# Expert routing placed later in each step, and layer 0's deviations taken from the attention's variance

## The chip, the cores and the metric

The kernel runs on one core of a Trainium2 chip. The time is the device time of one execution in microseconds (us); of several runs the median is given. The engines are TensorE (PE in the rows, PEld for its weight loads), VectorE (DVE), ScalarE (ACT), GpSimd (POOL) and SyncE (SP), each with a queue of its own that it works off in order; they wait for one another by semaphores.

## The reference

128 batches of 32 tokens with 128 channels go through three sublayers, each with a residual sum: a cross-attention to 257 context tokens (16 heads), a self-attention over the 32 tokens (16 heads), and a stack of four mixture-of-experts layers. The last is what the change touches:

```
def moe_layer(x, rw, rb, g, b, w1, b1, w2, b2):      # 4 experts, hidden 512, top 2
    logits = x @ rw + rb
    vals, idx = top_k(softmax(logits), 2);  vals = vals / vals.sum()
    xhat = (x - mean(x)) * rsqrt(var(x) + 1e-5)
    h = gelu((xhat * g[e] + b[e]) @ w1[e] + b1[e])
    y = h @ w2[e] + b2[e]
    return sum over chosen e of vals[e] * (x + y[e])
x = x2 + layers(layernorm(x2))                        # x2: what the self-attention leaves
```

Layer 0's input is itself a layer norm of x2: its mean is zero and its variance is that of x2 scaled by the square of the first inverse deviation.

## The kernel before

The 4096 tokens are 32 tiles of 128 (NT), eight blocks of four tiles (NBLK). The kernel has three parts one after the other, each an `nc.Block` whose end all engines wait for: cross-attention, self-attention, experts. All products with 16-bit operands are made of parts: a value is split into a high half and a low half (`xh` and `xl`, `gh` and `gl`, weights with parts 0 and 1), and three products make one.

The expert part runs over 32 steps (NSTEP): layer 0's eight blocks, then layer 1's, and so on. A step has four units e = 0 to 3, one for each expert. `steps` calls each engine's `unit(u, v, f, third, e, final)`: u is the current unit, v the unit before it (its second products and its combination are done one unit late), f the next step (what it needs is prepared now), third the step after that. The order of the calls in `unit` is the order of each engine's queue.

TensorE in a unit: `hidden(u)` (12 products of 512 columns, L1846); at e = 1 the transposes of the next step's normalised tokens (L1877); at e = 2 the twelve small routing products of the next step (L1887), which wait for `xl`; at e = 3 the second bias (L1896); then `outputs(v)` (48 products of 128 columns, L1863); at e = 1 the transpose of the combine weights (L1902).

ScalarE in a unit: four Gelus (L1666) and two copies to `gh` (L1671); at e = 1 `xh` (L1676); at e = 3 the tanh of the routing (L1690); in the first steps also `attended` (L1071), which writes the expert stack's input `hs` of one tile from the attention's output `xs`, and `high_weights` (L1036, L1039).

GpSimd makes half of `gl` (L1649), VectorE the other half (`low_half`, L1731).

VectorE in a unit: at e = 0 `normalise` (xc, L1719; in layer 3 also hs + xs, L1725); at e = 1 `deviations(third)` (statistics L1705 and L1709, then the inverse square root by three Newton steps, L38 to L53) and `xl` (L1812); `low_half(u)`; at e = 2 `route(f)` (L1755 to L1781, 14 small instructions in a chain, the last writes z); `combine(v)` (L1745, four instructions into hs); at e = 3 `add_bias` (L1801) and `weigh(f)` (L1784 to L1794). In steps 1 to 6 two experts' weights are split (`low_weights`, L1046 and L1050), behind e = 2 and e = 3, and TensorE waits ahead of step 7 (`ready`) until all are. (`outputs(v)` of e = 3 runs in the next step's e = 0.)

At the end of the self-attention part VectorE takes the statistics of the first eight attended tiles (`st8`, `mv8`), normalises the first block, splits the weights of experts 0 and 1, and then runs `attended_late` (the attention's deviations of the last eight tiles, L1426 to L1429) and the bias sum b1c (L1435).

## Time and profile before

| what | value |
|---|---|
| runs | 1383.1, 1382.77, 1380.51 us; median 1382.77 |
| profiled execution | 1380.24 us |
| its span, first to last instruction | 1378.5 us |
| mean granted TensorE clock | 0.97 |
| TensorE busy | 1270.3 us (92%) |
| VectorE busy | 1203.2 us (87%) |
| ScalarE busy | 1128.8 us (82%) |
| GpSimd busy | 714.0 us (52%) |

Busy times are shares of the whole span; which engine sets the end is read stage by stage. The expert part begins near 630 us. All rows are of the one profiled execution, which is 2.5 us under the median of the runs.

### The profile page before, as it was taken

The numbers are of one execution on the slowest core, as the hardware profiler recorded it, in microseconds if no ns is written. First come the engines' busy times: TensorE is split into PE (matmuls) and PEld (weight loads), VectorE is DVE, ScalarE is ACT, GpSimd is POOL, SyncE is SP. The second block draws the span as 40 slices with busy tenths as digits, with TensorE's granted clock in tenths as the row PEclk, the third lists the DMA queues.
The fourth block names the chain that finished last, engine by engine and source line by source line (L and its number), as shares of the span: only waits on it lengthen the run. The fifth ranks groups of instructions, "written<-read, shape, count | busy, mean of one in ns | idle before, by whom it ended". The sixth has DMA issues, their size and how long they took to land. (4 is left out here: it accounts for less than half of the span.)

```text
span 1378.5 us, 41462 instructions
## 1 busy us (share of the span) xinstructions
PE 1270.3 (92%) x15611; PEld 966.0 (70%) x15611; DVE 1203.2 (87%) x3492; ACT 1128.8 (82%) x1931; POOL 714.0 (52%) x559
## 2 busy tenths in 40 slices
PE   5898999999997689997889979999999999999998
PEld 3576778777776578954567657777777777776776
DVE  4799989999998678977899979998999999999986
ACT  3598999999996656766899968888888888888886
POOL 7276777777776864542334333344333344444343
PEclk9999999999998679999999999999999999999999
DMA  5985676676663279820000000000000000000000
GB/s 157 240 217 156 191 184 183 188 189 183 191 183 86 49 198 209 216 53 1 2 2 2 2 1 2 2 2 2 2 2 2 2 2 2 2 10 17 10 17 17
DMA packets 196269, 109.41 MB, mean 79 GB/s; under 512 B 89740, under 2 KB 194028, under 8 KB 196076
## 3 DMA queue, kind: packets, MB, share of 16 engines
q1 hardware_dynamic: 122032, 84.65, 22.1%
q10 hardware_dynamic: 74044, 22.17, 7.3%
q8 instruction: 123, 2.02, 0.6%
q14 instruction: 70, 0.57, 0.2%
HBM read 67.62 MB, written 39.03 MB: 77 GB/s over the span
## 5 line engine op out<-in xcount | busy, mean ns | idle before, releaser
L1649 POOL TENSOR_TENSOR gl<-gf,gh 128x1024 f16<-128x1024 f32 x128 | 290.6, 2270 | 461.7 <-ACT gh L1671 461.7
L1666 ACT ACTIVATE gf<-pair,b1c 128x512 f32<-128x512 f32 x512 | 329.5, 680 | 77.1 <-PE pair L1846 76.9
L1863 PE MATMUL pair<-w2p,gh 128*128 128x128 f16 x4096 | 356.9, 219 | 4.3 <-DVE hs L1745 2.6
L1863 PE MATMUL pair<-w2p,gl 128*128 128x128 f16 x2048 | 349.7, 219 | 0.0
L1846 PE MATMUL pair<-xh,w1p 128*128 128x512 f16 x1024 | 328.3, 382 | 7.3 <-DVE w1p L1046 7.3
L405 POOL TENSOR_TENSOR pl<-p,ph 128x1024 f16<-128x1024 f32 x128 | 273.1, 2134 | 116.0 <-ACT ph L462 115.9
L1863 PEld LDWEIGHTS pair<-w2p,gh 128*128 128x128 f16 x4096 | 317.5, 98 | 20.8 <-DVE hs L1745 3.1
L1671 ACT ACTIVATE gh<-gf 128x1024 f16<-128x1024 f32 x256 | 270.6, 1057 | 23.6 <-ACT gf L1666 0.4
L1731 DVE SCALAR_TENSOR_TENSOR gl<-gf,gh 128x1024 f16<-128x1024 f32 x128 | 164.0, 1281 | 42.0 <-ACT gh L1671 41.5
L1863 PEld LDWEIGHTS pair<-w2p,gl 128*128 128x128 f16 x2048 | 200.3, 98 | 0.0
L1846 PE MATMUL pair<-xl,w1p 128*128 128x512 f16 x512 | 195.7, 382 | 0.0
L1846 PEld LDWEIGHTS pair<-xh,w1p 128*128 128x128 f16 x1024 | 100.9, 99 | 115.3 <-DVE w1p L1046 7.4
L461 ACT ACTIVATE p<-pair 128x512 f32<-128x512 f32 x256 | 158.0, 617 | 23.7 <-PE pair L867 21.2
L462 ACT ACTIVATE ph<-pair 128x512 f16<-128x512 f32 x256 | 160.2, 626 | 0.0
L769 DVE TENSOR_REDUCE mx<-pair 128x4 f32<-128x1024 f32 x128 | 154.0, 1203 | 1.5 <-PE pair L840 0.5
L1745 DVE SCALAR_TENSOR_TENSOR hs<-pair,comb,hs 128x128 f32<-128x128 f32 x512 | 143.0, 339 | 0.1
L890 PE MATMUL pair<-VX,ph 128*128 128x36 f16 x1024 | 92.2, 180 | 9.1 <-DVE sl L630 6.2
L890 PEld LDWEIGHTS pair<-VX,ph 128*128 128x128 f16 x1024 | 83.7, 97 | 20.7 <-issue 14.5
L891 PE MATMUL pair<-VX,ph 128*128 128x36 f16 x1024 | 91.5, 179 | 0.0
L892 PE MATMUL pair<-VX,pl 128*128 128x36 f16 x1024 | 91.5, 179 | 0.0
L820 PE MATMUL pair<-cT,WkT 128*128 128x512 f32 x128 | 72.4, 648 | 20.2 <-ACT cT L452 12.6
L867 PE MATMUL pair<-QS,KS 98*128 98x128 f16 x1024 | 82.8, 224 | 4.0 <-ACT ph L462 3.4
(252 smaller groups left out, 2458.0 us busy)
## 6 DMA issues: line engine op xcount, KB each, us to landing
KS<-k_parts_dram SPq DMA_DIRECT2D x64, 384.0 KB, 4.5
k_parts_dram<-kh SPq DMA_DIRECT2D x64, 256.0 KB, 3.3
cx<-in_ctx_dram ACTq DMA_DIRECT2D x30, 512.0 KB, 4.7
k_parts_dram<-kl SPq DMA_DIRECT2D x64, 128.0 KB, 3.6
w1p<-in_L_ffn_w_dram SPq DMA_DIRECT2D x8, 512.0 KB, 6.0
w2p<-in_L_ffn_w_dram SPq DMA_DIRECT2D x8, 512.0 KB, 8.0
QS<-q_parts_dram ACTq DMA_DIRECT2D x128, 24.0 KB
K<-k_parts_dram SPq DMA_DIRECT2D x8, 384.0 KB
```

The source lines that it names most:

```text
L405: pool.tensor_tensor(pl[n % 4][:, :, :], p32[n % 2][:, :, :], ph[n % 4][:, :, :], ALU.subtract).then_inc(pl_done, 1)
L461: act.activation(p32[n % 2][:, c, :], TB[:, c * 512:(c + 1) * 512], ACT.Exp)
L462: act.activation(ph[n % 4][:, c, :], TB[:, c * 512:(c + 1) * 512], ACT.Exp).then_inc(t_read[c], 1)
L769: dve.tensor_reduce(mx[n // PB % 2][:, :, n % PB], RB[:, :].rearrange("p (g k) -> p g k", g=G), AX.X, ALU.max, negate=True).then_inc(r_rea ...
L890: pe.matmul(o, p_hi, hi, start=(c == 0), stop=False)
L1649: pool.tensor_tensor(gl[u.m2][:, 0:h, :], gf[u.m2][:, 0:h, :], gh[u.m2][:, 0:h, :], ALU.subtract).then_inc(d_loP, 1)
L1666: act.activation(gf[u.m2][:, c, :], hb[c][:, :], ACT.Gelu, scale=1.0 / WS, bias=b1c[:, u.step.expert(u.e), c]).then_inc(d_g, 1)
L1671: act.activation(gh[u.m2][:, c - 1:c + 1, :], gf[u.m2][:, c - 1:c + 1, :], ACT.Copy).then_inc(d_hi, 1)
L1731: dve.scalar_tensor_tensor(gl[u.m2][:, h:FC, :], gf[u.m2][:, h:FC, :], 1.0, gh[u.m2][:, h:FC, :], ALU.mult, ALU.subtract).then_inc(d_loD, 1)
L1745: dve.scalar_tensor_tensor(t, yb[v.m2][:, k * D:(k + 1) * D], comb[v.step.m2][:, k, v.e:v.e + 1], t, ALU.mult, ALU.add).then_inc(d_acc, 1)
L1846: last = pe.matmul(hb[c][:, :], w1p[:, u.step.expert(u.e), part, c * P:(c + 1) * P].rearrange("p a f -> p (a f)"), x[k][u.step.m2][:, :], ...
L1863: last = pe.matmul(yb[v.m2][:, t * D:(t + 1) * D], g[:, c, t * P:(t + 1) * P], w2p[:, le, part, c, :].rearrange("p a h -> p (a h)"), start ...
```

## The change

1. **Order on TensorE.** At e = 2 the routing products stand behind `outputs(v)` and not ahead of it.
2. **Order on VectorE.** `combine(v)` stands ahead of `route(f)`.
3. **Layer 0's deviations.** VectorE no longer takes statistics of the attended tiles. `expert_scale` works the deviation out of the attention's variance and inverse deviation, for 24 tiles in step (7, 3) of the attention part, for the last 8 in step 2 of the experts. `normalise_first` makes xc from `xs` with one combined scale. `late_deviations` (the attention's own for the last 8 tiles) moves into step 1.
4. **Attended tiles.** Tiles 16 to 31 are written by VectorE (`attended_late`, four tensor_scalars at e = 3 of steps 2 to 5) and no longer by ScalarE; ScalarE does 0 to 15.
5. **xh and xl of step 0** are made inside the attention part.
6. **Weights.** One expert's weights are split a step, steps 1 to 12 (ScalarE behind e = 0, VectorE behind e = 3); TensorE waits for a layer's weights at its first block, and `ready` is gone.
7. **Last layer.** hs + xs is made by GpSimd behind its `gl` of e = 0.

```diff
+        def expert_scale(dve, own, base):
+            dve.wait_ge(e_ln, base)
+            dve.scalar_tensor_tensor(vE[:, own], mv3[:, own, 1], 1.0, rs3[:, own], ALU.mult, ALU.mult).then_inc(e_ln, 1)
+            dve.wait_ge(e_ln, base + 1)
+            dve.scalar_tensor_tensor(vE[:, own], vE[:, own], 1.0, rs3[:, own], ALU.mult, ALU.mult).then_inc(e_ln, 1)
+            dve.wait_ge(e_ln, base + 2)
+            inverse_deviation(dve, seed, rsE[:, own], rwE[:, own], rt3[:, own], vE[:, own], e_ln, base + 2)
+            dve.scalar_tensor_tensor(rrE[:, own], rs3[:, own], 1.0, rsE[:, own], ALU.mult, ALU.mult).then_inc(e_ln, 1)
+        def normalise_first(dve, n):
+            dve.wait_ge(e_ln, SCALED if 4 * n + 4 <= HEAD else LATE_SCALED)
+            wait(dve, d_xT, n)
+            for k in range(4):
+                t = 4 * n + k
+                dve.tensor_scalar(xc[:, k, :], xs[:, t, :], mv3[:, t, 0:1], rrE[:, t:t + 1],
+                                  ALU.subtract, ALU.mult).then_inc(d_x, 1)
...
                             if at == (NBLK, 0):
-                                dve.wait_ge(d_hs, 8)
-                                for k in range(8):
-                                    dve.bn_stats(st8[:, k, :], hs[:, k, :]).then_inc(d_ln, 1)
...
+                                normalise_first(dve, 0)
+                                for le in range(2):
+                                    dve.wait_ge(e_b1, le + 1)
+                                    low_weights(dve, le)
+                            if at == (NBLK, 2):
+                                tokens_low(dve, 0)
...
                     blocks(step, prepare)(dve)
-                    dve.wait_ge(c_st, 2 * NT)
-                    attended_late()
...
-                        if splits and split and e in split_units:
-                            split(eng, 2 * cur.n + (E - 2 + split_units.index(e)))
+                        if split and cur and 1 <= cur.n <= LE - E and e == split_unit:
+                            split(eng, E - 1 + cur.n)
...
+                        if u and f and final and e == 0:
+                            blk = slice(4 * f.block, 4 * f.block + 4)
+                            pool.wait_ge(d_x, 4 * f.n + 4)
+                            pool.tensor_tensor(hs[:, blk, :], hs[:, blk, :], xs[:, blk, :], ALU.add).then_inc(d_sum, 1)
...
+                    def attended_late(n):
+                        dve.wait_ge(e_ln, LATE_R if 4 * n + 4 > HEAD else HEAD + RSTD_STEPS + 1)
+                        for t in range(4 * n, 4 * n + 4):
+                            dve.tensor_scalar(hs[:, t, :], xs[:, t, :], mv3[:, t, 0:1], rs3[:, t:t + 1],
+                                              ALU.subtract, ALU.mult).then_inc(d_hs, 1)
...
                         if u and f and e == 0:
-                            normalise(f, final)
-                        if u and third and e == 1 and not opening:
+                            if f.layer == 0:
+                                normalise_first(dve, f.n)
+                            else:
+                                normalise(f)
+                        if third and e == 1 and third.layer:
                             deviations(third)
...
-                        if opening and e == 2:
-                            deviations(third)
+                        if v:
+                            combine(v)
                         if f and e == 2:
                             route(f)
-                        if v:
-                            combine(v, final)
                         if u and e == 3:
                             add_bias(u.step)
                         if at == (0, 1):
                             low_weights(dve, 3)
+                        if at == (1, 2):
+                            late_deviations()
+                        if at == (2, 2):
+                            expert_scale(dve, slice(HEAD, NT), LATE_R)
+                        if u and e == 3 and 2 <= u.step.n < 6:
+                            attended_late(u.step.n + 2)
...
-                    steps(dve, unit, low_weights, (2, 3), lead=True)
+                    steps(dve, unit, low_weights, 3, lead=True)
...
+                        if v:
+                            outputs(v)
                         if f and e == 2:
...
-                        if v:
-                            outputs(v)
...
-                    def weights_ready():
-                        pe.wait_ge(e_lo1, LE)
-                        pe.wait_ge(e_lo2, LE)
-                    steps(pe, unit, ready=weights_ready)
+                    steps(pe, unit)
```

## Rows read from the trace of the kernel before

**Rows 1.** Windows: busy us and instructions of each engine, granted clock, DMA
```profile
640.00:820.00 180.00, 159.93 (x1812) 113.99 (x1810) 160.49 (x498) 153.88 (x232) 66.56 (x29) 0.98 0.01 2
820.00:1176.00 356.00, 355.88 (x4129) 260.04 (x4127) 325.71 (x1029) 308.04 (x433) 140.69 (x65) 1.00 0.01 2
1176.00:1378.00 202.00, 192.41 (x2250) 141.21 (x2247) 176.63 (x523) 164.24 (x230) 81.08 (x35) 1.00 0.04 12
```

**Rows 2.** Waits of TensorE from 600 us: total, times, longest
```profile
PE pair L1887 <- DVE xl L1812: 14.0, 14, 5.9
PE pair L1846 <- DVE w1p L1046: 7.3, 1, 7.3
...
PE pair L1863 <- DVE hs L1745: 2.6, 1, 2.6
```

**Rows 3.** Timeline, L1902 alone: start, us, instruction, idle before it
```profile
642.54 0.23 PE L1902 MATMUL pair<-ident,c 128*128 128x128 f16 x1 [1.52 <-DVE c L1794]
...
667.62 0.22 PE L1902 MATMUL pair<-ident,c 128*128 128x128 f16 x1
...
717.88 0.22 PE L1902 MATMUL pair<-ident,c 128*128 128x128 f16 x1
...
788.39 0.22 PE L1902 MATMUL pair<-ident,c 128*128 128x128 f16 x1
...
820.75 0.22 PE L1902 MATMUL pair<-ident,c 128*128 128x128 f16 x1
...
842.84 0.22 PE L1902 MATMUL pair<-ident,c 128*128 128x128 f16 x1
...
1176.92 0.22 PE L1902 MATMUL pair<-ident,c 128*128 128x128 f16 x1
...
1360.47 0.22 PE L1902 MATMUL pair<-ident,c 128*128 128x128 f16 x1
```

**Rows 4.** Timeline around the start of the expert part, and one window
```profile
625.14 0.64 DVE L1426 BATCH_NORM_AGGREGATE mv<-st 128x2 f32<-128x6 f32 x8
...
628.30 0.26 DVE L1435 TENSOR_TENSOR b1c<-pair,cols 128x64 f32<-128x64 f32 x1
...
629.56 0.69 DVE L1812 TENSOR_TENSOR xl<-pair,xh 128x512 f16<-128x512 f32 x1 [0.53 <-ACT xh L1676]
...
630.31 0.21 PE L1887 MATMUL pair<-rwp,xh 128*128 128x4 f16 x2 [5.94 <-DVE xl L1812]
...
632.00:634.00 2.00, 2.00 (x6) 0.64 (x5) 1.83 (x10) 1.39 (x3) 0.00 (x0) 0.50 0.00 0
```

**Rows 5.** Timeline of VectorE and GpSimd in one step at the floor
```profile
852.28 1.93 DVE L1781 SCALAR_TENSOR_TENSOR z<-top,lg 128x16 f32<-128x16 f32 x1
...
855.16 1.21 DVE L1731 SCALAR_TENSOR_TENSOR gl<-gf,gh 128x1024 f16<-128x1024 f32 x1
...
858.13 1.57 DVE L1784 TENSOR_SCALAR sel<-sel 128x16 f32<-128x16 f32 x1
...
860.25 1.24 DVE L1719 TENSOR_SCALAR xc<-hs,mv,rs 128x128 f32<-128x128 f32 x4
...
852.04 2.13 POOL L1649 TENSOR_TENSOR gl<-gf,gh 128x1024 f16<-128x1024 f32 x1 [3.33 <-ACT gh L1671]
857.52 2.14 POOL L1649 TENSOR_TENSOR gl<-gf,gh 128x1024 f16<-128x1024 f32 x1 [3.36 <-ACT gh L1671]
```

**Rows 6.** Timeline of VectorE in step 6: deviations and the second split
```profile
787.25 0.86 DVE L1705 BATCH_NORM_STATS2 st<-hs 128x6 f32<-128x128 f32 x4
...
790.92 0.69 DVE L1812 TENSOR_TENSOR xl<-pair,xh 128x512 f16<-128x512 f32 x1
...
806.14 0.74 DVE L1046 SCALAR_TENSOR_TENSOR w1p<-w1p,gain 128x512 f16<-128x512 f32 x1
...
807.41 1.11 DVE L1719 TENSOR_SCALAR xc<-hs,mv,rs 128x128 f32<-128x128 f32 x4
```

**Rows 7.** Timeline of VectorE in layer 3: the sum with xs
```profile
1173.22 0.69 DVE L1725 TENSOR_TENSOR hs<-hs,xs 128x512 f32<-128x512 f32 x1
```

More of the change, by code:

```diff
@@ L1060, in build @@
         e_rwh, e_b2, e_ln = sem("e_rwh"), sem("e_b2"), sem("e_ln")
[L1061 to L1063 removed]
+        vE, rsE, rwE, rrE = (sb(whole, f"rsE_{i}", [P, NT], F32) for i in range(4))
+        xh = [sb(whole, f"xh{i}", [P, 4 * P], F16) for i in range(2)]
+        xl = [sb(whole, f"xl{i}", [P, 4 * P], F16) for i in range(2)]
         warm = sb(whole, "warm", [P, 1], F32)
@@ L1526, in _ @@
                     blocks(step)(pe)
-                    pe.wait_ge(d_x, 4)
-                    pe.wait_ge(c_oc, NT)
-                    for k in range(4):
-                        last = pe.transpose(bank[6][:, k * P:(k + 1) * P], xc[:, k, :], ident[:, :])
-                    last.then_inc(d_xT, 1)
                     pe.wait_ge(e_cols, 5)
@@ L1590, in __init__, with steps, run @@
                     self.step, self.e, self.n, self.m2 = step, e, step.unit + e, e % 2
-            def steps(eng, unit, split=None, split_units=(0, 2), ready=None, lead=False):
-                SPLITS = (LE - E) // 2
-                def run(it, c, final, prepare=True, attend=True, splits=False, moments=lead):
+            def steps(eng, unit, split=None, split_unit=0, lead=False):
+                def run(it, c, final, prepare=True, attend=True, moments=lead):
                     cur = Step(eng, it, c) if attend else None
@@ L1620, in steps @@
                 run(0, 0, False)
-                for s in range(1, 1 + SPLITS):
-                    run(0, s, False, splits=True)
-                if ready:
-                    ready()
-                for s in range(1 + SPLITS, NSTEP - 2):
+                for s in range(1, NSTEP - 2):
                     run(0, s, s >= LAST - 1)
@@ L1738, in combine @@
                         dve.wait_ge(d_comb, v.step.n + 1)
-                        if final and v.e == 0:
-                            due = v.step.n - LAST + 2
-                            dve.wait_ge(d_sum, min(due, NBLK) if isinstance(due, int) else due)
+                        if v.step.layer == 0 and v.e == 0:
+                            dve.wait_ge(d_hs, 4 * v.step.n + 4)
+                        if v.step.layer == L - 1 and v.e == 0:
+                            dve.wait_ge(d_sum, v.step.block + 1)
                         for k in range(4):
@@ L1839, in hidden @@
                             pe.wait_ge(d_xl, u.step.n + 1)
-                        if isinstance(u.n, int) and u.n in (2, 3):
-                            pe.wait_ge(e_lo1, u.n + 1)
+                        if u.step.block == 0:
+                            pe.wait_ge(e_lo1, E * u.step.layer + u.e + 1)
                         x = (xh, xl, xh)
@@ L1852, in outputs @@
                         le = v.step.expert(v.e)
-                        if isinstance(v.n, int) and v.n in (2, 3):
-                            pe.wait_ge(e_lo2, v.n + 1)
+                        if v.step.block == 0:
+                            pe.wait_ge(e_lo2, E * v.step.layer + v.e + 1)
                         for c in range(FC):
@@ L1878, in unit @@
                             last.then_inc(d_xT, 1)
+                        if u and e == 3:
+                            if f:
+                                pe.wait_ge(d_xl, f.n + 1)
+                            pe.wait_ge(d_cc, u.step.n + 1)
+                            pe.matmul(tbk[:, :], cT16[:, :], b2R[:, bass.ds(u.step.layer, 1), :].rearrange("p a m -> p (a m)"),
+                                      start=True, stop=True).then_inc(d_P, 1)
+                        if v:
+                            outputs(v)
                         if f and e == 2:
```

137 lines of the change are left out of this document (59 added, 78 removed).

## The prediction

> **What bounds the kernel now.** I read the busy time by stretch first, then who waited for whom on TensorE, then the starts of one TensorE instruction that occurs once a step, and last the VectorE, GpSimd and ScalarE rows of one step. The expert stage (step 0 to step 31, four expert units a step) is TensorE's: between 820 and 1176 us it is busy 355.9 of 356 us, while VectorE has 325.7 [rows 1]. Before and after that it is not full: 159.9 of 180 us in layer 0, 192.4 of 202 us from layer 3 to the end [rows 1]. The longest waits of TensorE are all put down to VectorE [rows 2].
>
> The transpose of the combine weights (L1902) gives the step times [rows 3]. From 842.84 to 1176.92 it is 15 steps, 22.27 us each: TensorE's own work, the floor. Layer 0, 642.54 to 842.84, takes 200.3 us for 8 steps, 22.1 over their floor of 178.2. Step by step: 25.08 for step 0 (2.8 over), 50.26 for steps 1 and 2 (5.7 over), 70.51 for 3 to 5 (3.7 over), 32.36 for step 6 (10.1 over), about 0 for step 7. Layer 3, 1176.92 to 1360.47, takes 183.55, 5.4 over. So 27.5 us is all that VectorE's schedule costs, and the change can't win more there. The start of the stage is a second place: the attention block ends with VectorE's late deviations (625.14 to 628.3) and bias sum, and TensorE's first routing product waits 5.94 us for xl until 630.31; its clock is then granted at 0.50, the 1.2 GHz level, until 634 at least [rows 4].
>
> **The start.** The change takes `attended_late` out of the block's end: 625.14 to 628.30, 3.2 us on VectorE [rows 4]. It puts in `expert_scale` (15 instructions of 0.2 to 0.25: 3.0 to 3.7 us) and moves both `low_weights` and the first normalisation ahead. By the order in the code VectorE then reaches the last tile's transpose some 2.5 us later than now, the b1 products follow it, and the bias sum ends near 625.8 instead of 628.56. Since xh and xl of step 0 are now made inside the block, the 629.56 xl [rows 4] leaves the path: the routing product comes some 0.35 us after the bias sum, near 626.2, 4.1 us earlier. The gap ahead of it shrinks from 5.9 us to about 1 us, so the clock should stay at 2.4 GHz; at 0.50 it cost half of 630.3 to 634, about 2 us of products. ScalarE has one weight split ahead of its first Gelu instead of a split and four tiles. The first L1902 waits for VectorE's c16 now and will again. I take 6 us earlier for it (bounds 4.5, and 7.4 with the clock's 2 us and the ScalarE work counted in full).
>
> **The order in a step.** In a step at the floor the row of z (L1781) lasts 1.93 us, from 852.28 to 854.21, and GpSimd's gl runs 852.04 to 854.17; sel (L1784) lasts 1.57, from 858.13 to 859.70, and the next gl ends at 859.66 [rows 5]. Alone, each takes 0.2. So VectorE's small instructions are held until GpSimd's subtraction is over, some 3.1 us a step. The Trainium skill says this as a rule (SBUF — State Buffer, "Who interferes with whom"): a VectorE instruction with two SBUF inputs or in a two-port mode and a GpSimd instruction block each other for the whole instruction; the rows agree.
>
> Now put `combine` (1.04 us) ahead of `route` (2.7 us of work). Routing starts near 850.8, GpSimd starts at 852.04, the rest of the chain is held to 854.2 and ends near 855.2. The two together end where they end now (low_half starts at 855.16), because routing meets the same hold; only z is 1.0 us later. Tanh waits for it, the next Gelu comes 0.5 us late, with it GpSimd's gl and the end of sel's hold. xc (L1719), at 860.25 now, then starts near 860.7 and ends near 861.9; TensorE wants it at about 862.0. So the reordering alone costs nothing in a step without extras: I take 0.1 us for each of steps 13 to 23, +1 (bounds 0, and 4 if the 0.5 shows in most steps). What it wins is the wait for xl at the routing product (14.0 us over 14 waits, 5.94 of them the first [rows 2]), since the product now comes 2.7 us later, and step 0's 2.6 us wait for hs, where routing and deviations stood ahead of combine.
>
> **Layer 0.** From steps 0 to 5 the deviations go (787.25 to 790.92: 3.7 us each [rows 6]) and one of two weight splits (806.14 to 807.41: 1.27 us [rows 6]). Added: `late_deviations` in step 1 (3.1 us, as 625.14 to 628.30 less nb), `expert_scale` in step 2 (3.0), and in steps 2 to 5 `attended_late`, four tensor_scalars like xc, 1.04 us. In sum VectorE has 4 us a step less to do. But what is added stands at e = 2 and 3, ahead of low_half(3) and xc, and the deviations left from e = 1, where VectorE then waits for ScalarE. So the position counts, not the sum:
> - Step 1: routing ends near 854.8 in the times of the row step, late deviations 857.9, low_half(3) 859.0; TensorE wants it at about 858.1, then xc one split later: 2.0 us lost.
> - Step 2: expert_scale ends as gl starts and low_half(3) is held to 859.7: 2.9 lost, then attended_late and split put xc 2.0 later: 4.9.
> - Steps 3 to 5: attended_late stands where sel stands, at 858. If held like sel it ends at 860.5, then weights 0.75 and split 1.27 put xc at 862.5 to 863.6: 1.6 lost. If it slips through, 0.6. I take 1.5, since the held sel is a tensor_scalar too [rows 5]: 4.6 for three.
> - Steps 6 and 7: deviations are back, with one split: xc at 860.7 + 1.27 ends at 863.1: 1.0 lost each. But `ready`, the wait for all splits (7.3 us [rows 2], the 10.1 of step 6 with the slow clock after it), is gone, as weights are wanted a layer at a time.
> Sum with 0.3 for step 0: 13.8 against 22.1, so -8.3 (bounds: 4 lost if nothing is held, 19 if all is, so -18 to -3).
>
> **Steps 8 to 12** have a split each that they have not now: 5 x 1.0 = +5 (bounds 0, and 7 at more than the split's own 1.27).
>
> **Layer 3.** The sum with xs leaves VectorE: 0.69 us [rows 7], which is the 0.7 by which these steps exceed the floor. On GpSimd it is half of a 2.13 us instruction [rows 5], 1.07, right after xc, where it delays gl and holds VectorE's deviations by up to 0.4 to 0.8. I take 0.4 a step: 3.2 against 5.4, -2.2 (bounds 1 and 7 lost, -4.4 to +1.6). The Trainium skill speaks against this edit (GPSIMD Engine Reference, "Engine selection"): a two-input elementwise operation is about twice as slow there; by it the add would take 1.4 us and the gain would be near 1.
>
> **Sum.** -6 - 8.3 + 5 + 1 - 2.2 = -10.5 us against the profiled execution's 1380.24 (span 1378.5 and 1.7 around it), so 1369.7. The median of the runs is 1382.77, 2.5 above it; in that measure 1372.2.
>
> **Rivals.**
> 1. *VectorE's slack is real* (24 in 100): the added work slides into time in which VectorE would be held anyway, splits cost 0.3, steps 0 to 12 lose 8 in all. Then -7 at the start and 8 + 3 us left of 27.5, so -16.5: -23.5 in all, 1359 in the median's measure. For it: 4 us less work a step, and 325.7 of 356 us busy includes the holds. Against: steps 3 to 5 now lose 1.23 each (3.7 by three) with a plain chain of this kind.
> 2. *The split on the chain decides, slower* (8 in 100): the split now stands once between weigh and xc in steps 1 to 12 with nothing to hide it. At 1.0 a step it costs 12 us; if a step over the floor is also held longer at both places, it is 2.0 or more for steps 3 to 12, 20 us, plus 10 for steps 1 and 2 and 7 in layer 3: 37 against 27.5, less 5 at the start: 1387 (1380.2 + 4.5 + 2.5). It decides from 1.6 us a step.
> 3. *No change that shows* (8 in 100): the same losses as now, the start gains 3 and steps 8 to 23 give it back: 1382. Below 0.2% (2.8 us) a measurement of this kernel can't tell.
> 4. My own case, 1366 to 1379, has 60.
>
> **Numbers.** 1372. Eight in ten between 1357 and 1382. Faster by over 0.2%: my case and the first rival, 84 in 100; same 8; slower 8.
>
> **What would show it.** The first L1902 near 636.5; no wait of w1p on the first product of layer 0's last step; no wait of L1887 for xl; steps 1 and 2 at 24 to 27 us; steps 3 to 12 at 23 to 24 with the wait at L1877 for xc; 22.3 from step 13 on; 22.7 in layer 3, GpSimd's add near 1.07 us. I am wrong if steps 3 to 12 stand at 22.3 (rival 1) or above 24 (rival 2), or if routing is not held by gl in its new place.

## The result and the profile after

The changed kernel takes 1410.51 us (median of four runs, 1410.05 to 1413.83), the kernel before in the same job 1381.67 (1380.51 to 1383.1): a ratio of 1.0218, interval 1.02 to 1.0236. It is 28.8 us slower; 10.5 us faster was forecast.

The profiled execution has a span of 1408.3 us, 29.8 more than before. From the page of the changed kernel, its busy times and the group of GpSimd's gl (busy us, mean ns, idle before):

```profile
span 1408.3 us, 41350 instructions
...
PE 1281.9 (91%) x15611; PEld 977.5 (69%) x15611; DVE 1230.3 (87%) x3367; ACT 1119.5 (79%) x1915; POOL 731.6 (52%) x567
...
L1653 POOL TENSOR_TENSOR gl<-gf,gh 128x1024 f16<-128x1024 f32 x128 | 291.7, 2279 | 459.7 <-ACT gh L1680 459.7
```

The starts of the transpose of the combine weights (now L1924) answer to [rows 3]; they are steps 0, 1, 2, 3, 4, 5, 6, 8, 13, 23, 24 and 25. The last, step 31, is at 1390.28.

```profile
637.45 0.23 PE L1924 MATMUL pair<-ident,c 128*128 128x128 f16 x1 [1.67 <-DVE c L1811]
659.82 0.22 PE L1924 MATMUL pair<-ident,c 128*128 128x128 f16 x1
687.64 0.22 PE L1924 MATMUL pair<-ident,c 128*128 128x128 f16 x1
718.56 0.22 PE L1924 MATMUL pair<-ident,c 128*128 128x128 f16 x1
746.52 0.22 PE L1924 MATMUL pair<-ident,c 128*128 128x128 f16 x1
774.03 0.22 PE L1924 MATMUL pair<-ident,c 128*128 128x128 f16 x1
803.07 0.22 PE L1924 MATMUL pair<-ident,c 128*128 128x128 f16 x1
...
850.38 0.22 PE L1924 MATMUL pair<-ident,c 128*128 128x128 f16 x1
...
973.98 0.22 PE L1924 MATMUL pair<-ident,c 128*128 128x128 f16 x1
...
1200.74 0.22 PE L1924 MATMUL pair<-ident,c 128*128 128x128 f16 x1
1225.59 0.22 PE L1924 MATMUL pair<-ident,c 128*128 128x128 f16 x1
1248.44 0.22 PE L1924 MATMUL pair<-ident,c 128*128 128x128 f16 x1
```

Against the same steps of before: the start is 5.1 us earlier; steps 0 to 7 take 212.9 us (200.3 before), steps 8 to 12 123.6 (111.4), steps 13 to 22 226.8 (222.7), layer 3 189.5 (183.6). That is -5.1 + 12.6 + 12.2 + 4.1 + 6.0 = +29.8. Of these stretches only the start won. Within the first, step 0 (22.37 for 25.08) and step 6 (23.32 for 32.36) gained as forecast, and steps 1 to 5 lost more than that. The same four stretches as windows, and the waits in the expert part that matter (in all, times, longest), which answer to [rows 1, 2]:

```profile
637.45:850.38 212.93, 187.77 (x2065) 137.83 (x2066) 176.16 (x463) 164.60 (x240) 70.42 (x32) 0.95 0.01 2
850.38:973.98 123.60, 114.05 (x1294) 82.93 (x1292) 116.44 (x346) 99.98 (x144) 47.94 (x20) 0.99 0.01 2
973.98:1200.74 226.76, 224.36 (x2583) 162.57 (x2581) 211.65 (x643) 189.92 (x270) 95.14 (x41) 1.00 0.01 2
1200.74:1390.28 189.54, 178.08 (x2063) 130.00 (x2061) 174.78 (x489) 152.54 (x216) 86.51 (x40) 1.00 0.04 11
```

```profile
ACT th L1694 <- DVE z L1798: 34.9, 30, 1.4
...
PE pair L1885 <- DVE gl L1742: 22.4, 24, 3.9
...
PE pair L1899 <- DVE xc L1089: 15.6, 4, 4.2
PE pair L1899 <- DVE xc L1720: 10.5, 7, 3.3
```

The waits for xl and for w1p are gone, as forecast. In their place TensorE waits for gl (VectorE's low_half) and for xc, some of these waits 3 to 4 us long. No wait of TensorE or ScalarE names GpSimd's gl. The first row is ScalarE's: its tanh now waits for z in nearly every step, where before it did so twice (4.5 us in all). Step 4 (746.52 to 774.03) shows why the long ones are so long. Its timeline in order of time, of VectorE (the three small rows between sel and w1p are left out), GpSimd and the TensorE row that waited, and then the windows around it:

```profile
761.52 2.14 POOL L1653 TENSOR_TENSOR gl<-gf,gh 128x1024 f16<-128x1024 f32 x1 [3.80 <-ACT gh L1680]
761.78 2.73 DVE L1735 TENSOR_SCALAR hs<-xs,mv,rs 128x128 f32<-128x128 f32 x4
764.43 0.16 DVE L1801 TENSOR_SCALAR sel<-sel 128x16 f32<-128x16 f32 x1
...
765.15 0.74 DVE L1046 SCALAR_TENSOR_TENSOR w1p<-w1p,gain 128x512 f16<-128x512 f32 x1
765.81 0.68 DVE L1050 SCALAR_TENSOR_TENSOR w2p<-w2p 128x512 f16<-128x512 f32 x1
766.41 3.07 DVE L1089 TENSOR_SCALAR xc<-xs,mv,rsE 128x128 f32<-128x128 f32 x4
767.25 2.15 POOL L1653 TENSOR_TENSOR gl<-gf,gh 128x1024 f16<-128x1024 f32 x1 [3.59 <-ACT gh L1680]
...
769.54 1.11 PE L1899 MATMUL pair<-ident,xc 128*128 128x128 f32 x4 [3.89 <-DVE xc L1089]
```

```profile
766.00:768.00 2.00, 0.00 (x0) 0.00 (x0) 2.00 (x5) 1.91 (x4) 0.75 (x1) 1.00 0.00 0
768.00:770.00 2.00, 0.46 (x2) 0.46 (x3) 2.00 (x2) 1.38 (x2) 1.40 (x1) 0.73 0.00 0
770.00:772.00 2.00, 2.00 (x19) 1.93 (x18) 2.00 (x6) 0.60 (x1) 0.00 (x0) 0.50 0.04 8
772.00:774.00 2.00, 2.00 (x36) 2.00 (x34) 1.39 (x2) 0.00 (x0) 0.00 (x0) 0.92 0.00 0
```

GpSimd runs ahead of VectorE here: its gl of the next step's unit 0 starts at 761.52 and ends at 763.66, while VectorE is at the end of e = 3. The late attention outputs (L1735), 1.0 us of work, last 2.73: the first of the four is held. That was foreseen. sel, c16 and the split follow without a hold, and xc starts at 766.41. But ScalarE's chain doesn't wait for xc: it releases GpSimd's next gl, that of unit 1, which starts at 767.25, while the four instructions of xc are under way. They last 3.07 instead of 1.11. So xc is ready not 1.6 us late but 3.9 us, and after TensorE stood for these 3.89 us its clock is granted at 0.50, the 1.2 GHz level, in 770 to 772; the rows return to 0.92 in the next two. The step takes 22.27 + 3.89 + 1.35 = 27.51; the 1.35 is the rest, and the windows account for it: 2.00 us at 0.50, 2.00 at 0.92, and the 0.46 busy in the window before, if that was at 0.50 too, are some 1.4 us lost. In step 5 the clock is below 1.00 for longer and the rest is 2.9. Waits of 3.88, 3.13 and 3.68, 4.15, 3.89, 3.89 and 3.29 us stand in steps 1, 2, 3, 4, 5 and 12, and waits of 1.01 in step 6 and 1.24 in steps 7 to 11, where xc ends before the next gl starts (at 871.13, gl at 871.77, in step 8).

### The profile page after: what moved, and what is told of

Read it like the earlier page. It is cut to its first block, busy times and chain, and to the rows that moved or that the text cites. A ratio compares the mean times of both kernels' runs of the same rounds, so it can differ in the third digit from the quotient of the medians.

```text
span 1408.3 us, 41350 instructions
## 1 busy us (share of the span) xinstructions
PE 1281.9 (91%) x15611; PEld 977.5 (69%) x15611; DVE 1230.3 (87%) x3367; ACT 1119.5 (79%) x1915; POOL 731.6 (52%) x567
## 3 DMA queue, kind: packets, MB, share of 16 engines
q1 hardware_dynamic: 122032, 84.65, 21.6%
## 4 chain that ended last, share of the span: by engine, by line
DVE 20%; PE 19%; ACT 9%; issue 5%; POOL 1%; DVEq 0%; ACTq 0%
PE pair L1885 10%; PE pair L1868 8%; ACT gf L1675 5%; ACT gh L1680 4%; DVE hs L1756 3%; DVE ge L1785 2%; DVE gl L1742 2%; POOL gl L1653 1%; DVE xc L1720 1%; DVE sel L1801 1%; DVE xc L1089 1%; DVE gt L1788 1%; PE pair L1899 1%; DVE hs L1735 1%; DVE w2p L1050 1%
## 5 line engine op out<-in xcount | busy, mean ns | idle before, releaser
L1885 PE MATMUL pair<-w2p,gh 128*128 128x128 f16 x4096 | 367.3, 221 | 22.5 <-DVE gl L1742 22.4
L1675 ACT ACTIVATE gf<-pair,b1c 128x512 f32<-128x512 f32 x512 | 325.7, 677 | 63.0 <-PE pair L1868 62.4
L1885 PEld LDWEIGHTS pair<-w2p,gh 128*128 128x128 f16 x4096 | 324.4, 99 | 49.9 <-DVE gl L1742 26.6
L1885 PE MATMUL pair<-w2p,gl 128*128 128x128 f16 x2048 | 358.0, 221 | 0.0
L1680 ACT ACTIVATE gh<-gf 128x1024 f16<-128x1024 f32 x256 | 270.6, 1057 | 23.8 <-ACT gf L1675 0.7
L1742 DVE SCALAR_TENSOR_TENSOR gl<-gf,gh 128x1024 f16<-128x1024 f32 x128 | 171.0, 1336 | 40.8 <-ACT gh L1680 40.8
L1756 DVE SCALAR_TENSOR_TENSOR hs<-pair,comb,hs 128x128 f32<-128x128 f32 x512 | 143.2, 341 | 3.1 <-PE pair L1885 3.0
```

The lines of the kernel that those rows point to most:

```text
L1675: act.activation(gf[u.m2][:, c, :], hb[c][:, :], ACT.Gelu, scale=1.0 / WS, bias=b1c[:, u.step.expert(u.e), c]).then_inc(d_g, 1)
L1680: act.activation(gh[u.m2][:, c - 1:c + 1, :], gf[u.m2][:, c - 1:c + 1, :], ACT.Copy).then_inc(d_hi, 1)
L1742: dve.scalar_tensor_tensor(gl[u.m2][:, h:FC, :], gf[u.m2][:, h:FC, :], 1.0, gh[u.m2][:, h:FC, :], ALU.mult, ALU.subtract).then_inc(d_loD, 1)
L1756: dve.scalar_tensor_tensor(t, yb[v.m2][:, k * D:(k + 1) * D], comb[v.step.m2][:, k, v.e:v.e + 1], t, ALU.mult, ALU.add).then_inc(d_acc, 1)
L1885: last = pe.matmul(yb[v.m2][:, t * D:(t + 1) * D], g[:, c, t * P:(t + 1) * P], w2p[:, le, part, c, :].rearrange("p a h -> p (a h)"), start ...
```

## The experiments

Each was timed beside the kernel before on the same chip. Mean step time in us by stretch, from the starts of the transpose, for all of them (start is the first transpose, the last column the time from it to step 31's):

```
                start  1-2    3-5    6-7    8-12   13-22  23-30  step 0 to 31
before          642.5  25.13  23.50  27.23  22.28  22.27  22.94  717.9
after           637.5  29.37  28.17  23.65  24.72  22.68  23.69  752.8
a_extras_e1     640.3  28.76  23.57  24.36  24.42  22.73  23.69  738.2
a_attend_act    637.5  26.68  23.40  23.89  24.68  22.71  24.00  736.2
a_route_back    639.7  27.46  27.82  23.16  23.49  22.31  22.88  730.7
a_add_vector    641.2  28.00  28.25  23.66  24.72  22.68  24.00  752.9
a_half_gl       638.8  24.94  22.53  22.31  22.11  22.09  22.03  692.0
b_half_gl       642.5  24.72  22.52  26.11  22.09  22.09  22.03  700.6
b_order         644.6  25.12  23.99  27.76  22.79  22.72  23.97  736.8
a_two_gl        638.4  28.52  23.84  23.83  23.86  22.59  23.10  728.7
a_gl_13         635.9  26.62  23.51  24.04  24.04  22.87  22.64  724.0
best1           643.6  25.83  24.08  22.99  22.29  22.26  22.87  709.3
best2           638.5  25.83  24.08  22.99  22.28  22.26  22.19  703.8
best5           638.6  26.69  23.85  29.06  22.26  22.26  22.19  716.8
```

The start varies by several us among kernels whose code up to there is the same (best1 643.6, best2 638.5), so the parts are compared by their steps, and the medians are to be read with that in mind.

**a_extras_e1: the late attention outputs and VectorE's split to e = 1**

```
-  if u and e == 3 and 2 <= u.step.n < 6:
+  if u and e == 1 and 2 <= u.step.n < 6:
       attended_late(u.step.n + 2)
-  steps(dve, unit, low_weights, 3, lead=True)
+  steps(dve, unit, low_weights, 1, lead=True)
```

> The changed kernel with attended_late and VectorE's weight split moved from e = 3 to e = 1, behind combine, where VectorE stood idle 4.4 us in layer 0; the same work in all. Theory H (position and hold: work between routing and xc makes xc late, GpSimd's next gl then holds its four tensor_scalars some 2 us more, and a wait of 3.3 to 4.2 us halves TensorE's clock): steps 3 to 5 fall from 27.5 to 29 us to 22.3 to 23, step 2 from 30.9 to about 27; the span falls by 15 to 22, to about 1390 in the median. Rival S (the sum of VectorE's work decides, wherever it stands): within 3 us of 1410.

Measured: 1398.53 us (1396.86 to 1400.59), ratio 1.011 [1.0086, 1.0134]. Steps 3 to 5 fall from 28.2 to 23.6 with the same instructions on VectorE. The position decides there, not the sum. I had expected more: 22.3 to 23 in these steps, about 27 in step 2 (29.4 measured) and 1390 in all. In steps 6 to 11, where the deviations stand at e = 1 too, the split costs more there than behind e = 3 (24.3 to 24.4 a step, for 23.3 to 24.0); step 12 gives that back (24.5 for 27.7).

**a_attend_act: tiles 16 to 31 on ScalarE**

```
-  LATER = {(0, 3): (8, 12), (1, 3): (12, 16)}
+  LATER = {(0, 3): (8, 12), (1, 3): (12, 16), (2, 3): (16, 20), (3, 3): (20, 24), (4, 3): (24, 28), (5, 3): (28, NT)}
...
-  if u and e == 3 and 2 <= u.step.n < 6:
-      attended_late(u.step.n + 2)
```

with one small instruction more on VectorE, which makes ScalarE's bias for these tiles.

> The changed kernel with tiles 16 to 31 written by ScalarE again (one step's end each, steps 2 to 5), one small VectorE instruction more for their bias. H: without the 1.04 us of attended_late xc is out of the second hold, its wait falls from 3.9 to 1.2 and the clock stays up: steps 2 to 5 lose 3 to 5 us less each, 12 to 18 in all, about 1395. S: 4 x 1.04 = 4 us, 1406. If ScalarE's 1.6 us then makes tanh and the Gelus late: under 8 us gained.

Measured: 1393.45 us (1392.21 to 1394.35), ratio 1.0071 [1.0049, 1.0092]. Steps 3 to 5 take 23.4, step 2 24.6 instead of 30.9. Taking 1.0 us of work out of the chain ahead of xc gives 4.8 us a step. TensorE's wait for xc is 1.1 us in these steps instead of 3.9. By the rows of step 4 that is the work, the hold that it met, the second hold that it pushed xc into, and the clock.

**a_route_back: routing in its old order on both engines**

```
+  if f and e == 2:
+      route(f)
   if v:
       combine(v)
-  if f and e == 2:
-      route(f)
```

and on TensorE the routing product back ahead of the second unit's outputs.

> The changed kernel with the routing products ahead of outputs(v) and route ahead of combine again. H: z is ready 1 us earlier; steps 13 to 22 go back from 22.72 to 22.27 (-4.5), the split steps 8 to 11 from 23.99 to about 23.3, layer 0 changes by less than 5: 1397 to 1403. Rival R (the new order of routing is the main loss): 1385 or less.

Measured: 1389.98 us (1386.99 to 1395.27, six runs), ratio 1.004 [1.0013, 1.0068]. That is less than I had expected (1397 to 1403), and above the rival's 1385. Step 0 to 31 is 22 us shorter than in the changed kernel: of these four edits, each made alone, the reordering, which was priced at 1, gives most (16.6 for the tiles on ScalarE, 14.6 for the extras at e = 1, nothing for the sum below). The parts overlap, so these don't add up. Steps 14 to 22 are back at 22.27, steps 7 to 12 at 23.49 (one split on the chain: 1.22 each), layer 3 at 22.9. Steps 3 to 5 stay at 27.8, since the late outputs still push xc into the next gl (3.07 us again).

**b_order: the kernel before with this order alone**

> The kernel before with the order of routing alone changed: on VectorE behind the combination, on TensorE behind the second unit's outputs. Theory R (the order costs by itself): steps 13 to 22 take 22.72 instead of 22.27 (+4.5 us), steps 8 to 12 the same (+2), layer 3 at least +3 us, and the steps that also carry deviations and two splits more than 1 us each: 1393 to 1405. Rival (the order costs only together with the work that the change put behind it): under +4 us outside steps 0 to 7 and nothing within them: 1384 to 1388.

The edit is that of a_route_back the other way round. Measured: 1399.5 us (1395.9 to 1401.23), ratio 1.0113 [1.009, 1.0136]. Steps 13 to 22 stand at 22.72 and layer 3 at 24.0. So the order costs by itself, 19 us from step 0 to 31, but little in steps 1 to 5 (25.12 and 23.99), where I had expected more than 1 us each. What it does in a plain step shows in the changed kernel's rows of VectorE and GpSimd, which answer to [rows 5]:

```profile
1045.17 2.88 POOL L1653 TENSOR_TENSOR gl<-gf,gh 128x1024 f16<-128x1024 f32 x1 [3.56 <-ACT gh L1680]
...
1047.43 1.70 DVE L1742 SCALAR_TENSOR_TENSOR gl<-gf,gh 128x1024 f16<-128x1024 f32 x1 [0.34 <-ACT gh L1680]
...
1051.17 2.14 POOL L1653 TENSOR_TENSOR gl<-gf,gh 128x1024 f16<-128x1024 f32 x1 [3.12 <-ACT gh L1680]
1051.26 2.13 DVE L1785 TENSOR_TENSOR ge<-ge,lower 128x64 f32<-128x64 f32 x1
...
1057.37 2.13 POOL L1653 TENSOR_TENSOR gl<-gf,gh 128x1024 f16<-128x1024 f32 x1 [4.05 <-ACT gh L1680]
1057.63 1.90 DVE L1801 TENSOR_SCALAR sel<-sel 128x16 f32<-128x16 f32 x1
```

Before, two instructions of VectorE are held in a step, z and sel [rows 5]. Now there are three, ge, sel and a gl. The hold within routing meets its eighth instruction of fourteen instead of its last, so that 1.3 us of routing is left behind it. GpSimd's gl of unit 2 (1045.17) is held longer by VectorE's gl of unit 1 than before (2.88 us instead of 2.42), and then holds VectorE's gl of unit 2 (1.70 instead of 1.24). VectorE is busy 94.0 of 100 us in 1050 to 1150 (92.0 before, 91.3 in a_route_back), which is 0.9 us more in each step, with no work added. The combination isn't held: its four instructions (L1756) start at 1045.97, while GpSimd's gl is under way, and take 1.12 us as they do elsewhere.

Where TensorE loses the 0.45 us of a plain step can be read from its starts. In the kernel before it waits for xl ahead of the routing products, too shortly for its row to show it; in b_half_gl xl is done early and the same product comes 2.64 us after the step's transpose instead of 2.81:

```profile
1045.38 0.69 DVE L1812 TENSOR_TENSOR xl<-pair,xh 128x512 f16<-128x512 f32 x1
...
1046.13 0.20 PE L1887 MATMUL pair<-rwp,xh 128*128 128x4 f16 x2
```

The new order takes this 0.17 away. In its place the second products of unit 1, which wait for VectorE's gl behind the late chain, take 3.1 us instead of 2.7, and the transposes that want xc come 0.2 later:

```profile
1046.11 0.28 PE L1885 MATMUL pair<-w2p,gh 128*128 128x128 f16 x2 [0.26 <-DVE gl L1742]
```

**a_add_vector: the last layer's sum back on VectorE**

```
+  if final:
+      dve.wait_ge(d_x, 4 * f.n + 4)
+      dve.tensor_tensor(hs[:, blk, :], hs[:, blk, :], xs[:, blk, :], ALU.add).then_inc(d_sum, 1)
```

and GpSimd's sum is taken out.

> The changed kernel with the last layer's hs + xs on VectorE again. H: the alternation of 24.85 and 22.83 in layer 3 (mean 23.7 from step 23 on) is GpSimd's add pushing gl and its hold; with the add on VectorE the steps are even, 22.7 + 0.7 = 23.4 at most: 1 to 4 us less, 1406 to 1409. If the add on GpSimd is harmless: 1411 to 1415.

Measured: 1411.38 us (1409.33 to 1413.83), ratio 1.0196 [1.0174, 1.0219]: that of the changed kernel. That is the case where the sum on GpSimd is harmless. Layer 3 is no faster without GpSimd's sum (24.0), so this edit isn't what costs there, though each of the eight sums is twice as long as I took it (2.19 us in the mean):

```profile
1221.58 1.22 DVE L1742 SCALAR_TENSOR_TENSOR gl<-gf,gh 128x1024 f16<-128x1024 f32 x1
...
1221.74 2.19 POOL L1659 TENSOR_TENSOR hs<-hs,xs 128x512 f32<-128x512 f32 x1 [1.56 <-DVE xc L1720]
```

It starts 0.16 us behind VectorE's gl and is held until that ends at 1222.80; then it takes 1.13.

**a_half_gl: GpSimd's instruction on half its columns.** The direct test of the hold. The kernel leaves out half of GpSimd's low halves, which stay zero (set once before the steps); it is a test and no candidate. TensorE, ScalarE and VectorE issue what they issued.

```
-  pool.tensor_tensor(gl[u.m2][:, 0:h, :], gf[u.m2][:, 0:h, :], gh[u.m2][:, 0:h, :],
+  pool.tensor_tensor(gl[u.m2][:, 0:h, 0:2 * P], gf[u.m2][:, 0:h, 0:2 * P], gh[u.m2][:, 0:h, 0:2 * P],
                      ALU.subtract).then_inc(d_loP, 1)
...
+  for i in range(2):
+      pool.memset(gl[i][:, 0:FC // 2, 2 * P:4 * P], 0.0)
```

> The changed kernel with GpSimd's instruction of each unit working on half its columns (256 of 512 of both chunks; the other half of gl stays zero, so that part of the low halves is left out). TensorE, ScalarE and VectorE issue what they issued. Theory H (a small VectorE instruction is held until the 2.13 us GpSimd instruction ends, some twice, and TensorE then stands long enough for its clock to fall): the hold shrinks to about 1 us, the waits of 3 to 4 us in steps 1 to 5 and 12 fall under 2, steps 3 to 5 come down from 27.5-29.0 to under 25, steps 8 to 11 from 23.99 to some 22.5, steps 13 to 22 from 22.72 to about 22.3: some 25 us less in all, 1380 to 1390. Rival S (VectorE simply has too much work in the chain behind low_half, whatever GpSimd does): no step changes by more than 0.3 us, 1408 to 1412.

Measured: 1349.34 us (1348.07 to 1352.98), ratio 0.9761 [0.9736, 0.9787], 61.2 us less than the changed kernel (1410.51). I had expected some 25. A plain step now takes 22.09, less than the 22.27 that I had called TensorE's floor. The timeline of VectorE and GpSimd in its step 4, to be read against that of the changed kernel above:

```profile
747.63 1.99 DVE L1737 TENSOR_SCALAR hs<-xs,mv,rs 128x128 f32<-128x128 f32 x4
747.87 1.16 POOL L1653 TENSOR_TENSOR gl<-gf,gh 128x512 f16<-128x512 f32 x1 [4.30 <-ACT gh L1682]
...
751.52 1.11 DVE L1089 TENSOR_SCALAR xc<-xs,mv,rsE 128x128 f32<-128x128 f32 x4
...
753.60 1.19 POOL L1653 TENSOR_TENSOR gl<-gf,gh 128x512 f16<-128x512 f32 x1 [4.58 <-ACT gh L1682]
```

The first hold is 0.95 us instead of 1.7, xc is done a full microsecond before the next gl starts and isn't held, TensorE waits 0.21 us for it instead of 3.89, the clock doesn't fall, and the step takes 22.52 instead of 27.51. GpSimd's gl had 1% of the chain that ended last; halving it takes 4% off the kernel. The rival that a shorter gl helps only by being ready earlier doesn't stand: in the changed kernel neither TensorE nor ScalarE waits for GpSimd's gl.

**b_half_gl: the same in the kernel before**

> The kernel before with GpSimd's instruction of each unit on half its columns (the other half of gl stays zero and is left out), as was done to the changed kernel. This gives the fourth corner of a square: change without and with the long hold. Theory H (the change's price is the holds; apart from them it removes work): the steps of layer 0 stay above 22.1 here for their deviations and splits on the chain (23.5 to 24.5 in steps 1 to 6), all others fall to 22.1, and the kernel is slower than the changed one with the same halving (1349.3): 1355 to 1365. Rival (halving only gives all kernels VectorE time): 1340 to 1349, no slower than the changed one.

Measured: 1363.64 us (1360.91 to 1366.91), ratio 0.9876 [0.9854, 0.9898]. The square is complete:

```
                         before    after     change
GpSimd's gl whole        1381.67   1410.51   +28.8
GpSimd's gl halved       1363.64   1349.34   -14.3
what the long gl costs     18.0      61.2
```

(The 18.0 is against this table's 1381.67; in its own job before took 1381.21.) The time is in the range that I had expected, but steps 3 to 5 stand at 22.5, below it, so the work on the chain costs less there than I had thought. Without the long hold the change does what its parts are for. The changed kernel's steps 0 to 7 take 184.2 us against 193.0, -8.7, mostly by the wait for w1p that the kernel before still has in step 6 (30.1 us):

```profile
PE pair L1848 <- DVE w1p L1046: 6.3, 1, 6.3
```

The start is 3.7 earlier. From step 8 on, the two kernels with a halved gl are equal within 0.2 us: neither the order of routing nor a split on the chain in steps 8 to 12 costs anything there.

**a_two_gl: the same work of GpSimd, in two instructions**

```
-  pool.tensor_tensor(gl[u.m2][:, 0:h, :], gf[u.m2][:, 0:h, :], gh[u.m2][:, 0:h, :],
-                     ALU.subtract).then_inc(d_loP, 1)
+  for c in range(h):
+      pool.tensor_tensor(gl[u.m2][:, c, :], gf[u.m2][:, c, :], gh[u.m2][:, c, :],
+                         ALU.subtract).then_inc(d_loP, 1)
```

TensorE waits for the first before chunk 0 and for the second before chunk 1.

> The changed kernel with GpSimd's instruction of each unit cut in two, one of 128x512 for each chunk, nothing left out (GpSimd's work is the same, 2.3 us a unit instead of 2.14). Theory H1 (what costs is how long a single VectorE instruction can be held): VectorE gets in between the two, a hold is at most 1.2 us, and most of the gain of the halving comes: 1352 to 1370. Rival H2 (what costs is how long GpSimd is at work in all: the next VectorE instruction is held by the second half): a small instruction held by each half in turn costs as before, 1400 to 1412.

Measured: 1388.87 us (1384.19 to 1398.83, ten runs), ratio 1.0063 [1.0041, 1.0086]. That is outside both ranges, between the two: 21.6 us off the changed kernel, about a third of what the halving gave. VectorE does get in between the two halves, and then the next of its instructions is held by the second:

```profile
1056.25 2.32 POOL L1654 TENSOR_TENSOR gl<-gf,gh 128x512 f16<-128x512 f32 x2 [2.98 <-ACT gh L1681]
...
1056.48 1.06 DVE L1786 TENSOR_TENSOR ge<-ge,lower 128x64 f32<-128x64 f32 x1
1057.57 1.09 DVE L1789 TENSOR_TENSOR gt<-gt,ge 128x64 f32<-128x64 f32 x1
```

So shortening the single instruction gives part of the gain. That the rest is GpSimd's time in all is read from these rows alone.

**a_gl_13: one chunk for GpSimd, three for VectorE**

```
-  h = FC // 2
+  h = 1
```

on both engines, with TensorE's wait for VectorE's part ahead of chunk 1; nothing is left out.

> The changed kernel, complete, with GpSimd making the low half of chunk 0 alone (128x512, about 1.16 us) and VectorE those of chunks 1 to 3 (128x1536, about 1.8 us instead of 1.22). VectorE gets 2.3 us of work more in a step and loses up to four times 1 us of hold. Theory H: the holds weigh more than the work, since VectorE with half the hold had 1.8 us of slack in a step: steps of 22.1 to 22.7 outside steps 1 to 6, 1360 to 1380. Rival S (VectorE's sum of work decides): a step is then bound by VectorE at some 22.7 to 23.5, 1385 to 1420.

Measured: 1384.56 us (1380.43 to 1387.41, ten runs), ratio 1.0025 [1.0013, 1.0037]. It misses both ranges, 4.6 us above mine and 0.4 below the rival's, and its plain step is the rival's. This speaks for VectorE's sum of work counting too, which no run isolates. Even so, the 0.55 us more of work on each of VectorE's gl (1.76 instead of 1.22) weighs less than the shorter hold: 29 us less from step 0 to 31 than in the changed kernel, but 32 more than with the halved gl. A plain step takes 22.78; TensorE then waits for VectorE's gl, 29.4 us in 33 waits.

**best1 and best2: extras where VectorE stands idle.** best1 has the old order of routing and puts what the change added at e = 1, with two splits a step again; best2 also has the last layer's sum there, on VectorE.

```
-  if at == (1, 2):
+  if at == (1, 1):
       late_deviations()
-  if at == (2, 2):
+  if at == (2, 1):
       expert_scale(dve, slice(HEAD, NT), LATE_R)
-  if u and e == 3 and 2 <= u.step.n < 6:
-      attended_late(u.step.n + 2)
+  for n in {(3, 1): (4, 5), (4, 1): (6,), (5, 1): (7,)}.get(at, ()):
+      attended_late(n)
...
```

> The changed kernel with routing back in its old order on TensorE and VectorE, the deviations of tiles 16 to 31 and their scale at e = 1 instead of e = 2, the late attention outputs at e = 1 (blocks 4 and 5 in step 3, 6 in step 4, 7 in step 5), and again two splits a step in steps 1 to 6 (VectorE's behind e = 1 and e = 2). Theory: VectorE stands idle some 4 us ahead of its low_half of the third unit, so that work put there lies under TensorE, and no hold meets xc: steps 1 to 6 at 22.3 to 23.5, no stretch of lower clock, steps 7 to 22 at 22.27, layer 3 at 23.05; 1355 to 1362. Rival S (total VectorE work counts wherever it stands): steps 3 to 5 at 24 to 25, 1368 to 1375.

> The kernel of best1 with the last layer's hs + xs on VectorE behind the combination of e = 1 instead of on GpSimd behind its low half. If GpSimd's longer occupation at e = 0 is what holds layer 3 at 23.05 instead of 22.27, the steps of layer 3 take 22.3 to 22.5 and the time is 1350 to 1357; if not, they stay at 23 and the time is that of best1.

Measured: best1 1371.28 us (1368.17 to 1373.28), ratio 0.9911 [0.9887, 0.9936]; best2 1361.81 (1361.16 to 1365.02), ratio 0.9854 [0.9832, 0.9877]. best2 is the fastest complete kernel here: 48.7 us under the changed one. In layer 3 the sum's place is worth 5.4 us (22.87 to 22.19 a step): it is cheapest in VectorE's idle time at e = 1, neither on the chain nor on GpSimd. best1 is 9 us above the upper end of what was expected, best2 5. best1's time and its steps 3 to 5 (24.1 in the mean) lie in the rival's ranges, so extra work in VectorE's idle time isn't free either. Layer 3 was as expected in both; half of best1's miss is its start, 643.6 where the mean is 639.1. The rest is in steps 1 to 5, which take 23.7 to 25.9 and not 22.3 to 23.5. In step 4 of best2 TensorE waits 0.42 us (at 751.54) for the combination that routing, held for 2.18 us, delays, and 0.88 us (at 753.93) for the gl behind the split.

**best5: the second split to e = 0**

```
+  if at and e == 0 and 2 <= at[0] <= 7:
+      low_weights(dve, 2 * at[0] + 1)
+  if at and e == 1 and 1 <= at[0] <= 6:
+      low_weights(dve, 2 * at[0] + 2)
...
```

> The kernel of best2 with VectorE's second split of a step moved from behind e = 2 to behind the combination of e = 0 of the next step (steps 2 to 7), where VectorE stood idle 1.79 us ahead of xl in the trace of best2. In best2 TensorE waited 1.3 us for the combination of e = 1, which stood behind the routing and a held gl, and 0.9 us for the low half behind the split, in each of steps 3 to 5. Theory: with the split out of that chain these waits go: steps 3 to 5 at 22.3 to 23.0 instead of 23.7 to 24.8, steps 1 and 2 about 1 us less each, the rest as in best2: 1354 to 1358. Rival: the wait comes from the held instruction of routing alone, or the e = 0 split is held in turn and delays xl: 1360 to 1364.

Measured: 1376.55 us (1375.24 to 1377.15), ratio 0.9957 [0.994, 0.9973]: a miss, 14.7 us slower than best2. Steps 3 to 5 gain 0.2 us each, but step 1 loses 2.4, the split in its new place is held by the gl of unit 0, and in steps 6 and 7 the deviations of the next layer stand behind it, held in turn (30.0 and 28.1 us, for 23.4 and 22.6):

```profile
784.79 2.51 DVE L1046 SCALAR_TENSOR_TENSOR w1p<-w1p,gain 128x512 f16<-128x512 f32 x1
...
789.93 2.09 DVE L51 SCALAR_TENSOR_TENSOR rt<-rt,rw 128x4 f32<-128x4 f32 x1
...
794.18 0.22 PE L1912 MATMUL pair<-rwp,xh 128*128 128x4 f16 x2 [5.44 <-DVE xl L1100]
```

I had looked for idle time in one step's rows and had not asked what steps 6 and 7 put in the same place, nor whether gl runs there. It is the same mistake as the prediction's.

## Why the prediction was wrong

```
                   said    measured
start              -6      -5.1
steps 0 to 7       -8.3   +12.6
steps 8 to 12      +5     +12.2
steps 13 to 22     +1      +4.1
layer 3            -2.2    +6.0
sum               -10.5   +29.8
```

In one sentence: I priced VectorE's instructions at their place in the rows of the kernel before, and not against the next start of GpSimd's long instruction, which holds them. Half of the miss is in steps 0 to 7.

**The start** was right in mechanism and near in size: -5.1 against -6, the first transpose at 637.45 for 636.5. The bias sum ends at 626.22 and the first routing product comes at 626.53, for 625.8 and 626.2. The clock is granted in full (1.00 in 626 to 644). Over the eleven kernels with the change's attention part it is at 639.1 in the mean, over the three with that of before at 643.2, so -4 is the better figure, just outside the stated bound of 4.5.

**The w1p wait and the wait for xl** went as said: no row of either is left. That layer 0 gains 8.7 us with gl halved, for the -8.3 of the sum, is chance: 7.6 of it is step 6 alone, and step 2 loses 0.9 there.

**The order in a step** is the step of the prediction that failed first: "So the reordering alone costs nothing in a step without extras: I take 0.1 us". The changed kernel's plain step costs 0.45 more than before's (22.72 for 22.27), as does the order alone in the kernel before, and taking the order back from the changed kernel gives 22 of the 34.9 us that the expert part lost. I followed one hold, and routing did meet it; but I found the chain's end in the same place. z ends 1.4 us after GpSimd's instruction (1054.73 for 1053.31) and not 1.0, the next Gelu comes 0.8 us later against GpSimd's start and not 0.5, GpSimd's next gl starts 6.2 us after the last instead of 5.5, and VectorE's gl of unit 2 is now held as well. The xc of a plain step then comes some 0.2 us later than TensorE wants it, and the gl of unit 1 behind it costs 0.4. I put the bound at 0.5 us in most steps, which is the measured size, but took the lower end.

**Steps 3 to 5** failed most: 28.2 us where 23.8 was said. The place of the first hold was right: L1735, held, was to end at 860.5 of the row step's time, xc to be 1.6 us late. What failed is "then weights 0.75 and split 1.27 put xc at 862.5 to 863.6: 1.6 lost". It prices xc at its own 1.04 us. GpSimd's next gl is due about then, and isn't moved by xc's lateness, because ScalarE feeds it; an xc that is still under way then is held for 2 us more. So lateness isn't passed on one for one: up to about 1.2 us it costs itself (steps 8 to 11), beyond that it jumps to 3 to 4, and the clock after so long a stand costs 1.35 more in step 4 and 2.9 in step 5. Steps 1 and 2 have the same form. In step 1 the last instruction of the late deviations is held (1.98), which I had priced at its work, and TensorE stands 3.88 us for the gl behind it. In step 2 the last of expert_scale is held (2.05, as said), with low_half behind it, and then xc as well (3.03), which was not said. 5.6 and 8.7 us were lost for 2.0 and 4.9.

The Trainium skill has the rule behind it (SBUF — State Buffer, "Who interferes with whom"): of two instructions of VectorE and GpSimd that both need the shared port pair, the one issued first gets it for the whole instruction, and the other is blocked. The rows agree, in both directions: VectorE's small instruction until GpSimd's ends (2.13 for 0.22 of work), and GpSimd's gl and sum behind VectorE's gl (2.88 for 2.13, 2.19 for 1.13; each without a hold). I used the rule for the holds that the rows of before showed, and not for those that the change would make.

**Steps 6 to 12** were a term of the right kind and too small: 1.0 a step was said; 1.05 and 1.72 were measured for 6 and 7, 1.72 for 8 to 11, and 5.4 for step 12, where comb (2.00) and xc (3.07) are held as in step 4. In the old order one split on the chain costs 1.22.

**Layer 3** was said to gain 2.2 and lost 6.0. The steps alternate, 24.85 and 22.83, with a wait of 2.58 for a VectorE gl that is held (2.71 us) in every other one. The sum's move isn't the cause (a_add_vector); the order is (22.9 a step in a_route_back, 24.0 in b_order). I had priced GpSimd's sum at 1.07 by its work; it lasted 2.19, 1.06 of it held by VectorE's gl.

The second rival had the sign and its "if a step over the floor is also held longer at both places, it is 2.0 or more", but it placed the cost on the split. The runs put it on holds by GpSimd: with the halved gl the same splits on the same chain cost nothing in steps 8 to 12. It had 8 in 100; the row of 1.23 a step in steps 3 to 5, which the prediction names as the case against the first rival, was one more sign that these steps were at the edge.

**The floor.** The prediction called 22.27 us TensorE's own work. Both kernels with the halved gl take 22.09; the difference is the short wait for xl shown above.

Shown by runs: the share of the hold (the square), of the order (both directions), of the late outputs' place, and that GpSimd's sum costs no more than VectorE's at e = 0. Argued from rows alone: how the 0.9 us more of VectorE in a plain step divides among its holds, and the clock's share of a step. Not tried: the changed kernel with GpSimd's gl started at another time, which would test the meeting of xc and gl by itself. Why the start varies from kernel to kernel, by 5 us between best1 and best2 with the same code up to there, stays open.

## What to carry to other kernels

When two engines hold each other, an instruction's price depends on when it starts, and an engine with 1% of the chain that ended last can cost 4% of the kernel: before moving work, write down when the other engine's long instruction begins, what releases it, and which of your instructions would then be under way. A lateness is passed on one for one only until the next such start; past it the price jumps, and by then TensorE may stand long enough that its clock adds to it. Judge a place for extra work over all steps that use it. Halving GpSimd's work showed the most that the holds can cost here (61 us), but it leaves out part of the result. Of the complete kernels, the old order with the extras at e = 1 gave 48.7 us, cutting the long instruction in two 21.6 and moving half of it to VectorE 26. Both together were not tried.

## What the runs showed of the hardware

- GpSimd's four instructions of 2.13 us a step, 8.5 of 22.3 us, cost 18 us beyond their halves in the kernel before and 61 in the changed one.
- Not every VectorE instruction is held by GpSimd's: routing's small ones, sel, the split, xc and gl were (up to 3.07 us for 1.11), the combination wasn't (1.12 us for its four under a running gl).
- A plain step took 22.27 us with TensorE busy 99.99 of 100 us in 1050 to 1150, and 22.09 with it busy 100.00 when gl was halved: a wait of 0.17 us a step, 0.8%, didn't show in the busy share.
- After TensorE had stood 3.13 us (step 2, until 705.98) the granted clock stayed at 1.00 in 706 to 708, also after 2.58 us in layer 3. After 3.29 us (step 12, until 969.18) it was 0.57 in 970 to 974; after 3.88 and 3.68 us it was 0.54 and 0.57 in the next whole window, after 3.89 us 0.50:

```profile
706.00:708.00 2.00, 2.00 (x28) 1.65 (x29) 1.89 (x7) 0.00 (x0) 0.00 (x0) 1.00 0.00 0
970.00:972.00 2.00, 2.00 (x25) 2.00 (x23) 2.00 (x9) 0.53 (x1) 0.00 (x0) 0.57 0.00 0
```
